# First chunk's queries by transfers inside SBUF, batch 0's maxima by one-hot products, weight loads started earlier, and a new order

## What is computed

```
xn = layernorm(x)
x  = x + attention0(xn) + lora_experts(xn)
xn = layernorm(x)
x  = x + attention1(xn) + gated_ffn(xn)

attention0: q = xn Wq (32 heads of 16), k, v = xn Wk, xn Wv (one head of 16, shared)
            p = softmax(q k^T / 4 + slope_h * (pos_k - pos_q), causal);  out = (p v) Wo
lora_experts: 4 experts of rank 16, the best 2 by a softmax gate
attention1: per token, a 16 x 16 softmax over features; its result is repeated over 32 heads
gated_ffn: silu(xn G^T) * (xn U^T), then D; width 1792, integer weights with a scale per row
```

## Time and profile before

| | |
|---|---|
| time, median of 3 runs | 624.78 us (624.44 to 625.1) |
| span of the profiled execution | 623.2 us |
| its own time | not listed beside it; the median lies 1.6 us over the span |
| TensorE busy | 570.7 us (92%) |
| VectorE busy | 461.3 us (74%) |
| ScalarE busy | 377.0 us (61%) |
| POOL busy | 351.7 us (56%) |
| memory read, written | 30.19 MB, 8.39 MB |

### The profile page before, as it was taken

The page is one execution under the profiler, slowest core; times in us unless marked ns, Lnnn a source line. Parts: engine busy times, 40 slices in busy tenths (PEclk is TensorE's granted clock), DMA queues, the critical chain, the costliest instruction groups (busy, mean ns, idle before and its releaser), DMA issues.

```text
span 623.2 us, 14286 instructions
## 1 busy us (share of the span) xinstructions
PE 570.7 (92%) x5590; PEld 421.3 (68%) x5590; DVE 461.3 (74%) x1034; ACT 377.0 (61%) x703; POOL 351.7 (56%) x364
## 2 busy tenths in 40 slices
PE   4579583699999999999999999999999999999997
PEld 4466451467885668776968587858685876785783
DVE  4769874899999874899697748996986569354642
ACT  3287095847875478675757485858684776651240
POOL 6231595724655667674837574848576677542140
PEclk9987895599999999999999999999999999999999
DMA  8767799905054146001610160016001000000000
GB/s 207 152 95 78 123 237 217 170 2 54 2 54 87 37 68 70 3 4 35 88 17 5 35 86 4 4 35 88 1 5 52 18 1 9 28 2 2 35 1 34
DMA packets 98942, 34.97 MB, mean 56 GB/s; under 512 B 75548, under 2 KB 90044, under 8 KB 98876
## 3 DMA queue, kind: packets, MB, share of 16 engines
q1 hardware_dynamic: 76044, 24.58, 22.7%
q0 software_dynamic: 2352, 7.18, 5.7%
q10 hardware_dynamic: 20480, 2.31, 2.6%
HBM read 30.19 MB, written 8.39 MB: 62 GB/s over the span
## 4 chain that ended last, share of the span: by engine, by line
PE 68%; DVE 13%; SPq 8%; ACT 4%; issue 3%; DMA 2%; POOL 2%; ACTq 1%; DVEq 0%
PE B_bank L1266 27%; PE B_bank L1287 14%; PE A_bank L1218 7%; SPq L693 5%; PE A_bank L1191 4%; DVE mx L1537 4%; PE A_bank L1120 3%; PE E_bank L1176 3%; PE B_bank L1154 3%; PE E_bank L1171 2%; PE B_bank L1254 1%; DMA qq<-nmp 1%; ACTq L693 1%; SPq L731 1%; SPq L717 1%
## 5 line engine op out<-in xcount | busy, mean ns | idle before, releaser
L883 POOL TENSOR_TENSOR probs<-e,probs 128x512 f16<-128x512 f32 x176 | 208.3, 1188 | 127.2 <-ACT probs L999 126.8
L1266 PE MATMUL B_bank<-xs,wgu 128*128 128x256 f16 x1792 | 204.3, 273 | 0.3 <-DVE hf L1649 0.3
L998 ACT ACTIVATE e<-E_bank,wn 128x512 f32<-128x512 f32 x192 | 133.7, 696 | 103.4 <-PE E_bank L1176 53.9
L1266 PEld LDWEIGHTS B_bank<-xs,wgu 128*128 128x128 f16 x1792 | 172.7, 98 | 21.6 <-DVE hf L1649 0.6
L999 ACT ACTIVATE probs<-E_bank,wn 128x512 f16<-128x512 f32 x192 | 134.0, 698 | 0.0
L1287 PE MATMUL B_bank<-wd,hbuf 128*128 128x512 f16 x448 | 99.9, 379 | 0.1
L897 POOL TENSOR_TENSOR hbuf<-hf,hbuf 128x512 f16<-128x512 f32 x56 | 65.8, 1176 | 56.2 <-ACT hbuf L1033 55.8
L1537 DVE TENSOR_REDUCE mx<-B_bank 128x2 f32<-128x384 f32 (+5 forms) x168 | 92.1, 603 | 4.5 <-PE B_bank L1154 4.4
L1639 DVE SCALAR_TENSOR_TENSOR hf<-ebuf,B_bank 128x512 f32<-128x512 f32 x56 | 38.3, 684 | 62.2 <-ACT ebuf L1043 61.9
L1287 PEld LDWEIGHTS B_bank<-wd,hbuf 128*128 128x128 f16 x448 | 43.2, 98 | 49.3 <-POOL hbuf L897 0.6
L1043 ACT ACTIVATE ebuf<-B_bank,sgx 128x256 f32<-128x256 f32 x112 | 47.5, 485 | 22.1 <-PE B_bank L1266 20.8
(11 more groups left out here) (199 smaller groups left out, 696.3 us busy)
## 6 DMA issues: line engine op xcount, KB each, us to landing
qq<-q_parts SPq DMA_DIRECT2D x21, 256.0 KB
x<-in_x SPq DMA_DIRECT2D x20, 256.0 KB, 3.1
out_y<-x SPq DMA_DIRECT2D x16, 256.0 KB, 2.0
xa<-in_x SPq DMA_DIRECT2D x12, 256.0 KB, 5.1
q_parts<-qs SPq DMA_DIRECT2D x48, 64.0 KB, 2.9
wgu<-in_gate_w POOLq DMA_DIRECT2D x4, 448.0 KB, 9.1
wgu<-in_up_w POOLq DMA_DIRECT2D x4, 448.0 KB, 8.7
wd<-in_down_w POOLq DMA_DIRECT2D x4, 448.0 KB, 7.1
```

Source lines behind the costliest of these rows:

```text
L883: pool.tensor_tensor(probs[:, u % PSLOTS, 1, :], e32[:, w, :], probs[:, u % PSLOTS, 0, :], ALU.subtract).then_inc(s_lop, 1)
L998: act.activation(e32[:, w, :], psum("exp", i, g, w)[:, :], ACT.Exp, scale=wn[:, 7:8])
L1266: mm = pe.matmul(psum(name, u, i)[:, a * SEQ:(a + 1) * SEQ].rearrange("p (t n) -> p t n", t=NU), wgu[:, m, k, (2 * i + a) * P:(2 * i + a + ...
```

## The change

- The first chunk's q goes from `q_first` by transfers inside SBUF (`place` on SP: three a tile and batch, 512 bytes a piece) into a buffer `natural[m]` by head, and VectorE copies it from there into `qq` (`place` on DVE). The memory stores and gathers of the first chunk are gone.
- Batch 0's maxima don't go into rows of `qq`. They are made tile by tile (32 groups of two in place of 21), turned in two halves (`nm0`), kept as high and low in `nm_first`, and each score tile of batch 0 gets four further products that pick the right row of `nm_first` with a one-hot weight (`pick`) and add it in PSUM.
- The turned query weights lie in `xs`, not in `wgu`; the eight gate and up loads wait for nothing and are planned from 10 us on; the four down loads and the second layer's small loads wait for the last `place`. Gate and up have a semaphore of their own, down another.
- The mask and key tables are loaded between the first x tiles; the identity is taken from `identf`; the two position copies go from VectorE to ScalarE; ScalarE's table load is begun by a dummy exponential; `clear` goes from POOL to VectorE; `hi` and `lo` take the token weights first.
- All ranks are new.

The diff, cut to its core:

```diff
+FIRST_MAXG = [(tb, 2 * n, 2) for n in range(NK) for tb in range(NTB)]
+HI_ORDER = [NK, 0, 1, 2, 3] + list(range(NK + 1, 2 * NK + 2))
...
-    "PE": {"xT0": (-48.5, -1, 4), "tok": (-300.5, 0, 19, -10), "kT": (224, 0.5, -46, 146), "q0": (-50, 0.5, 13, -67),
+    "PE": {"xT0": (-381, -2, -104, 230), "tok": (-360.5, 1, -79, 20.5), "kT": (-280.5, 0.5, 30, -139.5), "q0": (585, 0),
...
-        wq_turned = wgu[:, :, :, :].rearrange("p a k n -> p (a k n)").bitcast(F32)[:, 0:NK * HID].rearrange("p (k n) -> p k n", k=NK)
+        wq_turned = xs_flat.bitcast(F32).rearrange("p (k n) -> p k n", k=NK)
+        natural = [wd[:, NB * NK:NB * NK + NK, :].rearrange("p i n -> p (i n)"), hf[:, :, :].rearrange("p a n -> p (a n)").bitcast(F16),
+                   attnT[:, :, :, :].rearrange("p a k t -> p (a k t)"), x1[:, NT:XSLOTS, :].rearrange("p a n -> p (a n)").bitcast(F16)]
...
+                    if c == 0 and t == 1:
+                        sp.dma_start(maskb, mask).then_inc(s_const, 16)
+                        sp.dma_start(mask_low, mask[0:P - R_HOT, :]).then_inc(s_const, 16)
+                        sp.dma_start(kst, k_cols).then_inc(s_const, 16)
...
-            def gather_first(m):
-                gather_heads(sp, 0, (m,), PART_Q, 0)
+            def place(b, m):
+                if b:
+                    sp.wait_ge(s_placed, m + 1)
+                for g, part in enumerate(PART_Q):
+                    if part == 0:
+                        sp.wait_ge(s_q0h, b * NK + m + 1)
+                    else:
+                        wait_used(sp, "q0", b, m)
+                    sp.dma_start(natural[m][g * HD:(g + 1) * HD, :].rearrange("d (h t) -> d h t", t=SEQ),
+                                 q_first[:, b, m, part, :]).then_inc(s_natural[m], 16)
...
             def late(n):
                 if n == 2:
-                    pool.wait_ge(s_nmrow[0], 32)
-                    pool.wait_ge(s_wlo, NK + 1)
+                    pool.wait_ge(s_placed, 2 * NK)
+                    pool.wait_ge(s_wlo, 1)
...
             def ffn_load(n):
                 k = n // 2
-                if n == 0:
-                    pool.wait_ge(s_gather[1], 16 * 3)
+                if n == 2 * NK:
+                    pool.wait_ge(s_placed, 2 * NK)
...
+            def tables():
+                act.wait_ge(s_rows, 96)
+                act.activation(pos_half, pos_nat, ACT.Copy)
+                act.activation(slope_up, slope_nat, ACT.Copy, scale=POS).then_inc(s_pos, 1)
...
-            def store(b, m):
-                wait_used(act, "q0", b, m)
-                store_heads(act, 0, b, m, q_first[:, b, m, :, :], s_q0[b][m])
...
+            def nm0(b, h):
+                wait_used(pe, "max", 0, 2 * NTB * (h + 1) - 1)
+                wait_free(pe, "nm0", b, h)
+                pe.transpose(psum("nm0", b, h)[0:NG // 2, 0:P], mx[:, 0, h * NG // 2:(h + 1) * NG // 2], identf[:, :])\
+                  .then_inc(full("nm0", b, h), 1)
...
+                pieces = 1 if w == 1 else 2
+                for piece in range(pieces):
+                    blocks = NTB // 2 // pieces
+                    c0, t0 = piece * blocks, (NTB // 2 if w else 0) + piece * blocks
+                    mm = pe.matmul(acc[:, c0:c0 + blocks, :, :], kk[:, b, piece, w, :], tokens[:, t0:t0 + blocks, :, :],
+                                   start=True, stop=i > 0, skip_group_check=True)
+                    for c1 in range(0 if i else blocks):
+                        row = g // 2 % 2 * 2 * NTB + 2 * (t0 + c1) + g % 2
+                        mm = pe.matmul(acc[:, c0 + c1, :, :], pick[:, row:row + 1].broadcast_to([NG, P]),
+                                       nm_first[:, g // (NHG // 2), :].rearrange("r (h t) -> r h t", t=GT), start=False, stop=True,
+                                       skip_group_check=True)
...
+            def place(b, m):
+                dve.wait_ge(s_natural[m], 48 * (b + 1))
+                dve.tensor_copy(qq[0:R_ALIBI, b, :, 8 * m:8 * m + 8, :],
+                                natural[m][0:R_ALIBI, :].rearrange("d (h c t) -> d c h t", c=NTB, t=GT)).then_inc(s_placed, 1)
...
+            def nm0(b, h):
+                dve.wait_ge(s_nm0, h + 1)
+                dve.scalar_tensor_tensor(out=nm_first[NG // 2:NG, h, :], in0=psum("nm0", b, h)[0:NG // 2, 0:P], scalar=-1.0 / NM,
+                                         in1=nm_first[0:NG // 2, h, :], op0=ALU.mult, op1=ALU.subtract).then_inc(free("nm0", b, h), 1)
```

More of the change, by code:

```diff
@@ L105 @@
               "att4": 1.4, "gate": 0.68, "up": 0.9, "down": 1.38},
-      "POOL": {"norm": 0.5, "norm2": 0.6, "lo": 1.3, "setup2": 2.2, "start": 2.0, "clear": 1.3, "turn": 1.0, "ffn_load": 0.62, "ln0": 1.0, "ln1": 1.0, "late": 0.75, "setup1": 0.5,
[1 row of a table added]
                "exp": 1.16, "att4": 2.3, "up": 1.2},
-      "SP": {"wo": 1.4, "x_load": 2.4, "consts": 5.0, "tables": 5.8, "q": 0.5, "gather": 2.1, "gather_first": 1.4, "nm": 1.2, "x1_load": 0.5, "down": 0.5}}
+      "SP": {"wo": 1.4, "x_load": 2.4, "consts": 7.5, "tables": 5.8, "q": 0.5, "gather": 2.1, "place": 1.4, "nm": 1.2, "x1_load": 0.5, "down": 0.5}}
@@ new lines @@
+    "POOL": {"start": (-90, 0), "ffn_load": (-158.5, 0), "ln0": (220, 0.5, 173, -85), "turn": (509.5, 0),
+        "norm": (127.5, 0), "late": (1694.5, 0), "norm2": (-257, 0), "lo": (-406.5, 0), "setup1": (-908, 0),
+        "setup2": (-456.5, 0), "exp": (-32, 0, 0, -371), "ln1": (-281, 3, -63.5, -117), "att4": (778, -1, 10.5, -159.5),
+        "up": (-495, -2, 15.5, -299)},
+    "SP": {"x_load": (-509, -2, 96, -372), "consts": (454, 0), "wo": (160.5, 0), "place": (338, 0), "tables": (-84, 0),
+        "q": (-702.5, 4, 100.5, 155), "gather": (856.5, 0, 23.5, -169.5), "nm": (648, 2, 1, -1), "x1_load": (-903.5, 0),
+        "down": (-856, 2, 428, 4)},
@@ L283, in attention @@
             u = 3 * (i * NHG + g) + w
[L284 removed]
+            p.add("PE", ("exp", i, g, w), *([] if w else [dve("nm0", 0, g // 4)] if i == 0 and g % 4 == 0 else [sp("nm", i, gap=2.8)] if i and g == 0 else []))
             after = [pe("exp", i, g, w)]
@@ L340, in query @@
         p.add("DVE", ("q0", b, m), act("q0", b, m))
-        p.add("ACT", ("store", b, m), dve("q0", b, m))
+        p.add("SP", ("place", b, m), dve("q0", b, m), *([dve("place", 0, m)] if b else []))
+        p.add("DVE", ("place", b, m), sp("place", b, m, gap=2.3))
     for m in range(NK if c else 0):
         n = c * NK + m
-        p.add("PE", ("qa", c, m), *[dve("xT0", c, t) for t in range(NT)], *([pool("lo", 3)] if c == 1 else []),
+        p.add("PE", ("qa", c, m), *[dve("xT0", c, t) for t in range(NT)], *([pool("lo", NK)] if c == 1 else []),
               *([pe("max", 2 * c - 3, 0)] if c > 1 else []), *([pe("tok", c, 1, gap=0.0)] if m == NK - 1 else []))
@@ L409, in plan @@
     for n in range(N_FFN):
-        p.add("POOL", ("ffn_load", n), sp("gather", 1, gap=8.0), at=34.0 + 5.0 * n)
+        p.add("POOL", ("ffn_load", n), *([pool("late", 8), dve("place", 1, NK - 1)] if n >= 2 * NK else []), at=10.0 + 1.0 * n)
     for c in range(NCH):
@@ L413, in plan @@
         if c == 0:
-            p.add("POOL", ("clear",), at=12.0)
             for m in range(NK):
@@ L428, in plan @@
             for n in range(9):
-                p.add("POOL", ("late", n), *([sp("nm", 0), pool("lo", NK)] if n > 1 else []), at=14.0)
+                p.add("POOL", ("late", n), *([pool("ffn_load", 2 * NK - 1), pool("lo", 0), dve("place", 1, NK - 1)] if n > 1 else []), at=14.0)
             for n in range(3):
@@ L436, in plan @@
                 p.add("DVE", ("scale2", n), pool("norm2", n), dve("scale"))
-            for n in range(10):
-                p.add("ACT", ("hi", n), dve("scale") if n < NK else dve("scale2", 0 if n == NK else 1))
+            for n, part in enumerate(HI_ORDER):
+                p.add("ACT", ("hi", n), dve("scale") if part < NK else dve("scale2", 0 if part == NK else 1))
                 p.add("POOL", ("lo", n), act("hi", n))
             p.add("DVE", ("setup0",), pool("late", 1, gap=6.0))
-            p.add("DVE", ("setup1",), pool("late", 8, gap=8.0), dve("nmT", 0))
+            p.add("DVE", ("setup1",), pool("late", 8, gap=20.0), dve("place", 1, NK - 1), dve("nm0", 0, 1))
             p.add("POOL", ("setup1",), dve("setup0"))
```

257 lines of the change are left out of this document (128 added, 129 removed), and 14 rows, old and new, of tables (RANK, US).

## The result

The change makes the kernel slower: 650.82 us (648.88 to 652.27) against 624.94 us for the kernel before on the same chip, a ratio of 1.040 (95% interval 1.0375 to 1.0427). The profiled execution has a span of 648.6 us, 25.4 more than before.

The account below looks back on a forecast made before the run. TensorE's work was taken to bound all after 116.42 us, idle time and slow clock the opening. VectorE's end put batch 1's first score at 98, 18.4 sooner; with 506.8 unchanged, span 604.8, forecast 606 us, range 598 to 614.

Parts of the forecast that it names:

- Weight loads sooner … not on the path.: Opening: eight loads start at about 10 us, not 68; gate needs weights late, so no cost on the path.
- the sign of failure: Opening: the q steps fail if the landing of the q transfers is over 7 us.
- the sum: Opening to batch 1's first score: engine ends give middle 98 us, 18.4 sooner; first maximum product at about 33.5.
- the q path: Opening: on-chip q costs 7.5 us a first tile, 11.5 with long landing; start some 16 us sooner than 49.24.
- Little: Rival, opening: the transfers decide, batch 1's first score comes at 106 to 115 us; 614 to 623.5 us, chance 0.20.
- The steps before it change little.: Start of the opening: steps before 22.8 us, where the scale of q is known, change little.
- The maxima's transfer: Batch 0, before its first score: two turns and two short copies, about 1.2 us, where 11.5 us passed.
- One-hots: Batch 0's scores: 96 added products take 7.3 us of TensorE, upper bound 11.3, hidden under ScalarE.
- VectorE, 75.8 us to the milestone.: Opening from 22.8 us: VectorE, nearest to full, has 75.8 us of work, ending at 98.6 to 108.0 less what slides.
- the milestone: Batch 1's first score product, at 116.42 us in the kernel before; forecast 92.6 to 102, middle 98.
- What follows keeps its 506.8 us.: Behind batch 1's first score: TensorE's own work, unchanged at 506.8 us.
- Slower: Rival, whole span: new order stalls later batches on maxima transfers, 4.5 us each, 638 us; over 626, chance 0.10.

Follow-up runs that it names:

- e1: The changed kernel with its eight gate and up loads issued later, behind the second weight low part in GpSimd's list; 645.36 us, ratio 1.031.
- e4: The kernel before with the eight gate and up loads issued early, the turned query weights in `xs` for that; 630.46 us, ratio 1.0075.
- e2: The changed kernel without batch 0's 96 one-hot products; 649.96 us, ratio 1.038.
- e14: e13 with one-hot weights and the maxima's high and low parts in 128 rows (lower 64 zero) instead of 64; 631.37 us, ratio 1.0086.
- e10: e9 without batch 0's one-hot products; 626.36 us, ratio 1.0022.
- e8: The changed kernel with the old order on every engine behind the planned start of batch 1's first score; 642.06 us, ratio 1.0245.
- e7: The changed kernel with only GpSimd's list reordered: low parts 0 to 4 first, then the all-reduce, loads later; 637.55 us, ratio 1.018.
- e9: The changed kernel with GpSimd's list reordered and the old order behind batch 1's first score; 631.14 us, ratio 1.0072.
- e11: e9 with GpSimd's loads and low parts of wo spread between batch 0's residuals; 636.46 us, ratio 1.0177.
- e13: e11 with gate and up loads before batch 1's maxima transfer, down loads moved, and four SyncE x loads behind it; 629.72 us, ratio 1.0038.
- e15: e13 with down loads behind batch 1's fourth pair of residuals and x loads behind the gather of batch 2's q; 630.61 us, ratio 1.0064.
- e16: e15 without batch 0's one-hot products; 628.09 us, ratio 1.0032.
- e19: e15 with VectorE's residuals of batch 0 cut from 512 to 32 columns from the third group on; 629.59 us, ratio 1.0059.
- e18: e15 without batch 0's one-hot products and with VectorE's residuals of batch 0 cut; 628.71 us, ratio 1.0042.
- e6: The kernel before with only the changed kernel's ranks (store, clear and first-gather steps keep their own); 653.87 us, ratio 1.043.

## Why the prediction was wrong

The forecast was 606 us, and 0.86 for faster; the measured time lies outside its range and on the other side. Step by step:

- **"Weight loads sooner … not on the path."** This step failed first. It asked whether the gate product needs the weights, and not what else the same engines carry at 12 to 45 us. The price that was put in, a landing of 7.2 us beside 3.2, was too small, and it priced the lesser part: SyncE couldn't issue the first `place` before 40.80, behind 11.31 and 14.26 us of issues for which the kernel before took 1.84 and 7.18, and its third transfer, issued by 42.74, was waited for until 51.01, 8.3 us, more than the 7 us that the prediction had named as the sign of failure. e1 and e4 show it from both sides. With late loads the first max product starts at 37.73, 10.1 us after that run's scale (27.60), where the sum had 10.7 (33.5 less 22.8), so the q path itself was costed well; the sum ran it beside traffic that it left out. The rule of the Trainium skill that the prediction quoted (DMA: Bandwidth & Descriptors, section Issuing engines are not separate DMA queues) agrees with these rows, and the rival "Little" that rested on it named the mechanism.
- **"The steps before it change little."** The scale came 9 us later. The third x tile is turned at 14.35 for 10.55, and TensorE's products for the scale start at 21.21 for 17.10. Then VectorE's new order puts the statistics of the second chunk's x ahead of the scale: from the end of GpSimd's power at 26.35 to VectorE's next step for the scale at 30.65 4.3 us pass, in which it waits 1.29 and 1.92 us for x, which lands after 11.8 us.
- **The maxima's transfer** fell from 11.5 to 2.1 us. Right.
- **One-hots**: 7.3 us with an upper bound of 11.3; they are listed with 13.7 us, and without them TensorE is busy 12.4 us less (e2, 575.7 for 588.1). The term took its price from products of 128 rows in a row; the change between 64 and 128 rows, which it left out, is 5.6 us of the stretch (e14). That they are hidden was right in the changed kernel (0.9 us) and wrong in the merged order (some 3 us, e10).
- **VectorE, 75.8 us to the milestone.** It took 73.7 from 31.84 on. That the size fits is in part chance: the eight copies took 7.3 us for 5.2, the residuals 965 ns each for 720, and 3.5 us of statistics had moved ahead of the scale. The conclusion that the milestone follows from the fullest engine was wrong: 129.94 for 98 (the middle of 92.6 and 102 is 97.3). VectorE stood idle in 14.3 us of the first 20, for the late q.
- **"What follows keeps its 506.8 us."** It took 518.7. With the old order behind the milestone it took 510.3 (e8): about 8 of the 12 us are order.
- **The ranks had no term in the sum.** This is the largest gap. They appeared as the rival "Slower" with a chance of 0.10, priced by waits for each later batch's maxima. The side was right and the place wrong: behind the milestone no wait for the transfer of maxima is among TensorE's nine longest, and the greater loss lies ahead of it, in GpSimd's list (e7: 0.022, of which e1's loads alone give 0.009) and only then in the tail (e8: 0.016).

Shown: loads and GpSimd's list, and the order of the tail, make about 20 of the 26 us (e9). Shown too: of the prices that remained under suspicion, the one-hots are worth some 3 us in e9's order (e10); clearing the maxima's transfer brings e11's 1.0177 back to 1.0038, some 2 us under e9 with overlapping intervals (e13), and clearing the gather's brings nothing (e15); and in e15's order leaving out the one-hots, cutting VectorE's residuals, or both, moves the ratio by 0.0032, 0.0005 and 0.0022, not clear of its noise (e16, e19, e18). So none of them alone explains the 0.6% that e15 still loses. Open is whether the two moves are worth anything by themselves. No run had an order made for them and free of these waits; the nearest, e13 and, with work left out, e10, e16 and e18, end 0.2 to 0.4% above the kernel before, and three executions of e13 ended below it for a reason that isn't known. The loss behind 110 us in e18 was located and not taken apart: that the old tail doesn't fit the sooner start is argued, not shown.

## What to carry to other kernels

A schedule written out for all engines belongs to its set of steps. Price a changed order as a term of its own, engine by engine: for each step that others wait for, look at what now stands ahead of it in its queue. A load that nothing needs early isn't free early: look at which small transfer on the path shares the queues with it. And before a gain at the front is carried to the end, name what the next stretch will wait for, since what e1, e11 and e13 won at the front was each time lost, all or in part, in the next wait. Last, read the price of a small product from the starts of its neighbours and not from its own mean, which hid a factor of two here (e14).

## What was not expected of the hardware

- The maximum over partitions on GpSimd is listed with 0.38 us and holds the engine for some 13. In GpSimd's timeline of the changed kernel nothing that it waited for is shown between 57.91, where VectorE's input for it is done, and 70.83 (in the kernel before, between 49.51 and 62.81):

```profile
56.52 1.15 POOL L845 TENSOR_TENSOR wq<-hbuf,wq 128x512 f16<-128x512 f32 x1 [0.53 <-ACT hbuf L958]
63.28 0.38 POOL L893 PARTITION_ALL_REDUCE cmax<-cmax  x1 [5.61 <-issue]
70.83 3.82 POOL L845 TENSOR_TENSOR wq<-hbuf,wq 128x512 f16<-128x512 f32 x3 [7.18 <-issue]
```

- Loads that GpSimd issues cost it more than is listed. In e1 eight of them, listed from 42.42 to 46.99, stand ahead of the same maximum over partitions, and 20.7 us pass from there to GpSimd's next work, where 12.9 and 13.3 pass without loads ahead.
- VectorE's residual of 512 columns took 720 ns in the kernel before and 1166 in e9 (60 to 130 us), and one other instruction 4.57 us in place of 0.49; the long ones lie between 74 and 94 us, where GpSimd worked without a gap. The Trainium skill, SBUF — State Buffer, section Who interferes with whom, which the prediction used for the other direction, speaks of such a shared port; that it is the port and not something else was not tried.
- TensorE's busy time for the same products isn't fixed: 570.7 us before and 582.2 in e6, which adds no product but only another order. The mean granted clock is 0.959 before and 0.942 in e6.
- Products whose weights change between 128 and 64 rows start 0.21 us apart, and 0.11 us apart with 128 rows throughout, for the same columns (e13 and e14).
